# Cross-attention and an RWKV block: outputs reordered by small copies instead of turnings on TensorE, and more pairs of steps with a weighing between the score tiles

## The chip, the cores and the metric

One core of one Trainium2 chip. The metric is the device time of one launch in microseconds, lower is better; it is the median of several runs.

## What is computed

Batch 8, 256 tokens, width 256. First a cross-attention with 32 query heads and 8 key/value heads (head size 8) over 1601 context tokens, with output projection, residual and layer norm:

```python
q = x @ Wq + bq;  k = ctx @ Wk + bk;  v = ctx @ Wv + bv
scores = einsum('bkgld,bksd->bkgls', q, k) / sqrt(8) + mask        # mask is zero here
out = einsum('bkgls,bksd->bkgld', softmax(scores), v)
x = layernorm(out.reshape(b, l, 256) @ Wo + bo + x) * gamma + beta
```

Then an RWKV block per batch element: layer norm, token shift, low-rank mixes, products r, k, v, g, a decayed state `s = k v + w s` scanned over the 256 tokens for 32 heads, group norm, projection, and a channel mix with a squared relu and a sigmoid gate.

## The kernel before, in words

The program is written out by hand for each engine, with semaphores between them. It is a pipeline over the batch elements. In turn `it` five elements are at work: `f = it + 2` (its keys and values are projected), `a = it + 1` (its stacks of queries and keys are made), `b = it` (its scores, exp and weighing run), `c = it - 1` (output projection and the RWKV block up to the scan), `d = it - 2` (the channel mix's end). A letter is None where the element does not exist: `c` in turn 0, `f` in turns 6 and 7, `b` from turn 8 on, which is the tail.

A turn has 52 steps: four groups of heads (`GROUPS`) by 13 chunks of 128 keys (`NC`). In a step PE makes two score tiles (128 x 1024 each, two matmuls of 512 columns), ACT takes the exp of each (`exp_tile`), and PE weighs the values with them (`weigh`), adding a group's 13 steps up in PSUM bank 4 (`po`), where a head lies in nine rows: eight of output, one of the denominator. There are two PSUM buffers for score tiles, so a score tile waits for the exp of the tile two before it. `weigh` of a group's first step waits until DVE has copied the group before out of the bank (`keep_output` into `o_raw`, semaphore `o_kept`).

PE works in pairs of steps. In an ordinary pair both score tiles of the first step are issued, then the weighings of the two steps before, then both tiles of the second step, then the pair's side work (`side`). In a pair that stands in `LIGHT` each weighing stands between two score tiles. Where `c` is None every pair but step 0 and the two in `DIVIDED` is light.

Side work of `c` that matters here: step 4 the output product w_o, 10 the turned `xn`, 16 Wv, 20 Wk, 24 Wr, 26 Wg, 34 the gather of the scan; of `f`: `project_kv` at steps 30, 32 and 40, whose results DVE biases (`bias_kv`, `kv_biased`). After each group, PE turns `o_raw` (`turn_output`: four 128 x 128 transposes, at steps 22, 28, 42 and at step 0 of the next turn), and DVE normalises the turned tile (`norm_output`: a reciprocal of 16 denominators a row, four small products into `attn`). At step 2 PE turns `attn` (`turn_rows`), DVE copies it to `attn_t`, and w_o is applied at step 4.

SP issues nearly all DMAs, in the order in which its program lists them: at step 0 `load_stacks(b, 1)` and `load_x_rows(c)`, at step 4 the stores of `a`'s query and key parts, at 14 the shift of group half 1 (`shift_to_dram`, `shift_to_stack`), at 18 `spread_v(c)` (eight DMAs of 257 KB from SBUF to SBUF), at 20 the context and x_t of `f`, at 26 `load_stacks(a, 0)`, at 38 the shift of half 0, at 44 the mask.

Before turn 0, element 0 is projected, its parts are split and stored to DRAM (`store_k_parts`, `store_queries`), read back as stacks (`load_stack_half`), and a sub-round of scores gives the shift of the exponent, which goes through DRAM too. SP loads the context of element 1 before it issues these stores. POOL loads the weights that are needed from turn 1 on (`late_loads`) as soon as element 0's context has come.

## Time and profile before

| | |
|---|---|
| runs | 1173.62, 1179.3, 1179.63 us; median 1179.3 |
| the profiled execution | 1178.83 us, of which 1176.9 between its first and last instruction |
| PE | 1054.9 us busy |
| ACT | 860.3 us busy |
| DVE | 574.8 us busy |
| POOL | 309.0 us busy |
| mean granted TensorE clock | 0.952 of full speed |
| moved by DMA | 87.48 MB |

An engine's busy time is the sum over its instructions; idle time of an engine that is not the bottleneck costs nothing. Lines such as L795 are lines of the kernel; most of PE's matmuls share L795, since a helper issues them, and are told apart by what they write and read.

### The profile page before, as it was taken

The numbers are of one execution on the slowest core, as the hardware profiler recorded it, in microseconds if no ns is written. First come the engines' busy times: TensorE is split into PE (matmuls) and PEld (weight loads), VectorE is DVE, ScalarE is ACT, GpSimd is POOL, SyncE is SP. The second block draws the span as 40 slices with busy tenths as digits, with TensorE's granted clock in tenths as the row PEclk, the third lists the DMA queues.
The fourth block names the chain that finished last, engine by engine and source line by source line (L and its number), as shares of the span: only waits on it lengthen the run. The fifth ranks groups of instructions, "written<-read, shape, count | busy, mean of one in ns | idle before, by whom it ended". The sixth has DMA issues, their size and how long they took to land.

```text
span 1176.9 us, 18264 instructions
## 1 busy us (share of the span) xinstructions
PE 1054.9 (90%) x7181; PEld 376.0 (32%) x7181; DVE 574.8 (49%) x1095; ACT 860.3 (73%) x940; POOL 309.0 (26%) x356
## 2 busy tenths in 40 slices
PE   3198999999999999999999999999997999888777
PEld 2031223333333233323333333323331333224413
DVE  5031215464448445555547453844555364635562
ACT  2078988889878887888788988887788888881110
POOL 9221051232314041314123231314132012300330
PEclk8599999999999999999999999999999999998766
DMA  8534133631536140904253143614070225000400
GB/s 258 128 82 134 25 83 86 93 83 57 116 44 136 59 95 30 170 6 94 83 87 88 58 113 44 139 59 93 31 107 3 34 75 82 3 1 9 72 0 13
DMA packets 65374, 87.48 MB, mean 74 GB/s; under 512 B 8208, under 2 KB 48192, under 8 KB 65280
## 3 DMA queue, kind: packets, MB, share of 16 engines
q1 hardware_dynamic: 61728, 81.22, 31.6%
q0 software_dynamic: 2176, 4.11, 1.5%
q8 instruction: 59, 0.97, 0.3%
q10 hardware_dynamic: 1376, 0.90, 0.3%
q14 instruction: 35, 0.29, 0.1%
HBM read 50.74 MB, written 18.62 MB: 59 GB/s over the span
## 4 chain that ended last, share of the span: by engine, by line
PE 62%; ACT 23%; issue 6%; DVE 5%; DMA 3%; SPq 1%; POOL 0%; ACTq 0%; DVEq 0%; POOLq 0%
PE psum L795 61%; ACT probs L738 19%; DMA vs<-v_c 1%; DMA q_stacked<-q_parts 1%; ACT L738 1%; ACT L770 1%; PE psum L885 1%; SPq L291 1%; DVE xa L1336 1%; DMA q_stack<-q_stacked 1%; DVE row_max L1248 1%; DVE sx L1341 0%; ACT xm L767 0%; ACT xm L770 0%; SPq L367 0%
## 5 line engine op out<-in xcount | busy, mean ns | idle before, releaser
L738 ACT ACTIVATE probs<-psum 128x1024 f32<-128x1024 f32 (+1 forms) x832 | 798.9, 1022 | 199.8 <-PE psum L795 197.5
L795 PE MATMUL psum<-probs,v_aug 128*9 128x512 f32 (+1 forms) x3328 | 416.7, 599 | 1.3 <-DVE o_raw L1296 1.2
L795 PE MATMUL psum<-q_stack,k_stack 64*128 64x512 bf16 (+1 forms) x1745 | 320.5, 395 | 50.2 <-ACT probs L738 37.9
L795 PEld LDWEIGHTS psum<-q_stack,k_stack 64*128 64x128 bf16 (+1 forms) x1745 | 81.9, 96 | 440.5 <-ACT probs L738 359.5
L795 PEld LDWEIGHTS psum<-probs,v_aug 128*9 128x9 f32 (+1 forms) x3328 | 61.6, 89 | 161.2 <-issue 151.3
L599 POOL TENSOR_TENSOR vs<-r_c,vs 128x512 f32<-128x512 f32 x64 | 86.5, 1361 | 96.4 <-DVE tmp L1523 53.9
L576 POOL TENSOR_TENSOR xm<-tmp,xa 128x512 f32<-128x512 f32 x40 | 43.5, 1104 | 233.2 <-DVE tmp L1356 233.2
L1369 DVE TENSOR_TENSOR_SCAN vs<-w_c,vs 128x514 f32<-128x514 f32 x64 | 90.1, 1408 | 21.8 <-POOL vs L590 19.9
L563 POOL TENSOR_TENSOR rstd<-moments,eps 128x2 f32<-128x2 f32 x24 | 4.7, 195 | 255.8 <-DVE moments L1322 255.8
L1296 DVE COPY o_raw<-psum 128x512 f32<-128x512 f32 x32 | 21.9, 684 | 89.7 <-PE psum L795 89.7
L1362 DVE TENSOR_TENSOR vs<-k_c,vs 128x512 f32<-128x512 f32 x64 | 61.9, 967 | 0.3
L1356 DVE SCALAR_TENSOR_TENSOR tmp<-psum,chan,sx 128x256 f32<-128x256 f32 x80 | 33.5, 478 | 53.3 <-PE psum L795 53.3
L795 PE MATMUL psum<-ctx_t,w_kv 128*128 128x400 f32 (+1 forms) x128 | 50.1, 529 | 5.4 <-DMA ctx_t<-in_ctx_t 5.4
L535 POOL CAST k_parts<-kv 64x1601 bf16<-64x1601 f32 x7 | 10.6, 1519 | 121.0 <-DVE kv L1225 121.0
L1248 DVE TENSOR_REDUCE row_max<-psum 128x16 f32<-128x512 f32 x32 | 20.6, 684 | 41.8 <-PE psum L795 41.8
L1225 DVE TENSOR_SCALAR kv<-psum,b_kv 128x400 f32<-128x400 f32 (+1 forms) x28 | 17.6, 627 | 42.5 <-PE psum L795 42.5
L795 PE MATMUL psum<-k_stack,q_stack 48*128 48x32 bf16 x512 | 9.0, 174 | 30.9 <-DMA q_stack<-q_stacked 30.9
L795 PEld LDWEIGHTS psum<-ctx_t,w_kv 128*128 128x128 f32 x128 | 23.3, 195 | 25.2 <-issue 11.1
L1566 DVE RECIPROCAL xm<-xm 128x512 f32<-128x512 f32 x8 | 26.8, 3348 | 7.1 <-ACT xm L770 7.1
L1242 DVE TENSOR_REDUCE mask_max<-ctx_t 128x1 f32<-128x1601 f32 x16 | 28.7, 1806 | 0.0
L795 PE MATMUL psum<-mix,w 128*128 128x256 f32 (+1 forms) x64 | 18.0, 415 | 6.2 <-DVE mix L1345 6.2
L1285 DVE CAST shift_parts<-psum 32x128 bf16<-32x128 f32 x16 | 4.5, 279 | 38.8 <-PE psum L795 38.8
(181 smaller groups left out, 1061.8 us busy)
## 6 DMA issues: line engine op xcount, KB each, us to landing
vs<-v_c SPq DMA_DIRECT2D x61, 257.0 KB, 7.6
ctx_t<-in_mask SPq DMA_DIRECT2D x8, 1601.0 KB, 6.7
k_stacked<-k_parts SPq DMA_DIRECT2D x48, 200.1 KB
ctx_t<-in_ctx_t SPq DMA_DIRECT2D x24, 400.0 KB, 6.1
k_stack<-k_stacked SPq DMA_DIRECT2D x31, 300.2 KB, 6.6
q_stack<-q_stacked SPq DMA_DIRECT2D x31, 192.0 KB, 7.1
q_stacked<-q_parts SPq DMA_DIRECT2D x90, 64.0 KB, 3.1
ctx_t<-in_ctx_t SPq DMA_DIRECT2D x8, 401.0 KB, 6.4
```

What stands on the lines that cost most here:

```text
L576: nc.gpsimd.tensor_tensor(xm[MIX_ORDER[n]][:, :, :], tmp[n % 2][:, :, :], xa[:, :, 1:L + 1], ALU.add)\
L599: nc.gpsimd.tensor_tensor(vs[:, j, :, 0:L], r_c[:, :, :], vs[:, j, :, 0:L], ALU.mult)\
L738: nc.scalar.activation(probs[turn_step % NP][t][0:w, :, :], ps[t][0:w, :, :], ACT.Exp).then_inc(exped.sem, 1)
L795: return nc.tensor.matmul(dst, lhsT, rhs, start=start, stop=stop)
L1225: nc.vector.tensor_scalar(kv32[:, at:at + w], bank(at_bank)[:, 0:w], b_kv[:, 0:1], None, ALU.add)\
L1242: nc.vector.tensor_reduce(mask_max[:, a, lc:lc + 1], ctx_t[:, lc, :], AX.X, ALU.max, apply_absolute_value=True).then_inc(mask_seen.sem, 1)
L1248: last = nc.vector.tensor_reduce(row_max[:, :].rearrange("p (r a u) -> p r a u", a=2, u=4)[:, :, half, :], bank(6 + half).rearrange("p (r ...
L1296: nc.vector.tensor_copy(o_raw[:, :], po).then_inc(o_kept.sem, 1)
L1356: last = nc.vector.scalar_tensor_tensor(tmp[n % 2][:, e, :], halves(at)[:, e, :], vec(f"s{f}", e), sx[:, e, :], ALU.add, ALU.mult)
L1362: nc.vector.tensor_tensor(vs[:, j, :, 1:L + 1], k_c[:, :, :], vs[:, j, :, 1:L + 1], ALU.mult)\
L1369: nc.vector.tensor_tensor_scan(flat, w_c[:, :, :].rearrange("p e l -> p (e l)"), flat, 0.0, ALU.mult, ALU.add)\
L1566: link(nc.vector.reciprocal(std_o[:, :, :], std_o[:, :, :]))
```

## The change

The turned outputs and their normalisation in rows are gone. Instead SP copies each group's `o_raw`, with eight DMAs from SBUF to SBUF, head by head to rows of `attn_t`, and the denominators, spread over eight rows each, to rows of `den_t` (`turn_attn`). They are issued at steps 22, 30 and 42, and at step 0 of the next turn, ahead of what else SP has in those steps and behind what it has in earlier ones. `keep_output` waits for the group before to have been copied. Once a turn DVE takes the reciprocal of all denominators, their minimum (in place of the denominators kept for `count_over`), and multiplies (`norm_attn`). w_o is loaded with its rows in the order of `attn_t`.

`LIGHT` has seven pairs more: 4, 20, 22, 28, 30, 44, 50. The load of `x_rows` moves from step 0 to step 46 of the turn before. At the start SP issues element 0's stores and stack load before the context of element 1, ACT takes two of SP's query stores over, and POOL starts the late loads only when the first stacks have landed. Waits of PE for `o_normed` become waits for what else uses the bank.

```diff
-LIGHT = (2, 8, 10, 18, 38, 42, 48)
+LIGHT = (2, 4, 8, 10, 18, 20, 22, 28, 30, 38, 42, 44, 48, 50)
+ATTN_STEP = (22, 30, 42)
+FIRST_STORES = 2
...
+            def turn_attn(b, group):
+
+                if group == 0 and b > 0:
+                    sp.wait_ge(wo_done.sem, wo_done.at(b - 1))
+                sp.wait_ge(o_kept.sem, o_kept.at(b, group + 1))
+                for j in range(4):
+                    p0 = 32 * group + HD * j
+                    for dst, src in ((den_t, o_raw[32 * j + HD:32 * j + HD + 1, :].rearrange("p (a n) -> p a n", a=1)
+                                      .broadcast_to([1, HD, 512])),
+                                     (attn_t, o_raw[32 * j:32 * j + HD, :])):
+                        sp.dma_start(dst[p0:p0 + HD, :, :].rearrange("p h l -> p (h l)"), src).then_inc(attn_in.sem, 16)
...
-                sp.wait_ge(kv_proj.sem, kv_proj.at(lo))
-                load_ctx(lo + 1)
-                sp.wait_ge(q_proj.sem, q_proj.at(lo))
-                load_x_t(lo + 1)
...
                 store_k_parts(lo)
-                store_q_parts(lo, (1,))
+                sp.wait_ge(q_low.sem, q_low.at(lo))
+                store_queries(sp, lo, 1, range(FIRST_STORES, NR))
                 load_stacks(lo, 0, (0,))
+                sp.wait_ge(kv_proj.sem, kv_proj.at(lo))
+                sp.wait_ge(q_proj.sem, q_proj.at(lo))
+                load_ctx(lo + 1)
+                load_x_t(lo + 1)
...
                         if step == 0:
+                            if c is not None:
+                                turn_attn(c, 3)
                             if b is not None:
                                 load_stacks(b, 1)
-                            if c is not None:
-                                load_x_rows(c)
+                        if step in ATTN_STEP and b is not None:
+                            turn_attn(b, ATTN_STEP.index(step))
+                        if step == 46 and b is not None:
+                            load_x_rows(b)
...
+                if lo == 0:
+                    pool.wait_ge(stack_in[0].sem, stack_in[0].at(0))
+                    for dst, src in late:
+                        pool.dma_start(dst, src).then_inc(late_in.sem, 16)
...
-                    if step == 0:
-                        pe.wait_ge(o_normed.sem, o_normed.at(c, 3))
-                        turn_output(c, 3, 5)
-                    elif step == 2:
-                        pe.wait_ge(o_normed.sem, o_normed.at(c, 4))
+                    if step == 4:
...
-                        turn_rows(attn, 5, attn_turned)
-                    elif step == 4:
-                        pe.wait_ge(attn_kept.sem, attn_kept.at(c))
+                        pe.wait_ge(attn_normed.sem, attn_normed.at(c))
                         product_rows(attn_t, w_o, 5, wo_done)
...
             def keep_output(b, group):
                 dve.wait_ge(weighed.sem, weighed.at(b, NC * (group + 1)))
-                dve.wait_ge(o_turned.sem, o_turned.at(b, group))
+                if group > 0:
+                    dve.wait_ge(attn_in.sem, attn_in.at(b, 16 * HD * group))
+                elif b > 0:
+                    dve.wait_ge(attn_in.sem, attn_in.at(b - 1))
                 nc.vector.tensor_copy(o_raw[:, :], po).then_inc(o_kept.sem, 1)
...
+            def norm_attn(b):
+
+                dve.wait_ge(attn_in.sem, attn_in.at(b))
+                nc.vector.reciprocal(den_t[:, :, :], den_t[:, :, :]).then_inc(den_turned.sem, 1)
+                dve.wait_ge(den_turned.sem, den_turned.at(b))
+                nc.vector.tensor_reduce(den_low[:, b % B:b % B + 1], den_t[:, :, :], AX.XY, ALU.min)
+                nc.vector.tensor_tensor(attn_t[:, :, :], attn_t[:, :, :], den_t[:, :, :], ALU.mult)\
+                  .then_inc(attn_normed.sem, 1)
...
-                        norm_output(c, 3, 5)
-                        dve.wait_ge(attn_turned.sem, attn_turned.at(c))
-                        nc.vector.tensor_copy(attn_t[:, :, :], halves(5)).then_inc(attn_kept.sem, 1)
+                        norm_attn(c)
```

## Rows read from the trace of the kernel before

**Rows 1.** The page's chain of work that ended last, shares by engine.
```profile
PE 62%; ACT 23%; issue 6%; DVE 5%; DMA 3%; SPq 1%; POOL 0%; ACTq 0%; DVEq 0%; POOLq 0%
```
**Rows 2.** Busy time of each engine in one turn's window; columns in its first row.
```profile
core 0: us, PE busy (x) PEld busy (x) DVE busy (x) ACT busy (x) POOL busy (x), PEclk, DMA share, GB/s
562.80:690.40 127.60, 123.71 (x887) 44.73 (x887) 69.80 (x135) 106.40 (x116) 34.84 (x36) 1.00 0.38 81
```
**Rows 3.** PE in order of time: start, duration (us), instruction, idle before it and its releaser.
```profile
612.23 0.66 PE L885 MATMUL psum<-ident,o_raw 128*128 128x128 f32 x4
...
623.13 1.90 PE L795 MATMUL psum<-probs,v_aug 128*9 128x512 f32 x16
...
634.79 1.61 PE L795 MATMUL psum<-ctx_t,w_kv 128*128 128x400 f32 x4
...
690.60 0.39 PE L795 MATMUL psum<-q_stack,k_stack 64*128 64x512 bf16 x2 [0.48 <-ACT probs L738]
...
693.78 1.99 PE L795 MATMUL psum<-w_o,attn_t 128*128 128x256 f32 x8
```
**Rows 4.** Groups by line and shape: busy us and mean ns, then idle before.
```profile
L1566 DVE RECIPROCAL xm<-xm 128x512 f32<-128x512 f32 x8 | 26.8, 3348 | 7.1 <-ACT xm L770 7.1
...
L1310 DVE TENSOR_TENSOR attn<-psum,r_den 128x32 f32<-128x32 f32 x128 | 15.5, 184 | 1.1
...
L1464 DVE TENSOR_TENSOR x<-x,rows 128x512 f32<-128x512 f32 x8 | 5.5, 692 | 0.3
```
**Rows 5.** SP in order of time, in turn 4: start and duration of DMA issues.
```profile
562.45 0.60 SPq L291 DMA_DIRECT2D q_stacked<-q_parts  x1
...
588.50 0.33 SPq L385 DMA_DIRECT2D shift_stacked<-shift_parts  x1
...
597.71 14.85 SPq L304 DMA_DIRECT2D vs<-v_c  x8
612.68 4.61 SPq L351 DMA_DIRECT2D ctx_t<-in_ctx_t  x4
617.33 0.86 SPq L354 DMA_DIRECT2D x_t<-in_x_t  x1
618.36 0.91 SPq L284 DMA_DIRECT2D k_stack<-k_stacked  x1
```
**Rows 6.** DMA issues in 563 to 691 us: KB each, us from issue to landing.
```profile
out<-y_out SPq DMA_DIRECT2D x1, 256.0 KB, 2.2
x_t<-in_x_t SPq DMA_DIRECT2D x1, 256.0 KB, 7.9
...
shift_stacked<-shift_parts SPq DMA_DIRECT2D x2, 24.0 KB, 1.4
```
**Rows 7.** DVE in order of time.
```profile
620.39 0.68 DVE L1296 COPY o_raw<-psum 128x512 f32<-128x512 f32 x1
...
634.04 0.61 DVE L1225 TENSOR_SCALAR kv<-psum,b_kv 128x401 f32<-128x401 f32 x1
...
683.19 0.69 DVE L1296 COPY o_raw<-psum 128x512 f32<-128x512 f32 x1 [4.39 <-PE psum L795]
```
**Rows 8.** PE in order of time, in turn 0.
```profile
94.12 1.90 PE L795 MATMUL psum<-probs,v_aug 128*9 128x512 f32 x8 [1.20 <-DVE o_raw L1296]
```
**Rows 9.** Window of 3 us behind it; columns as in rows 2.
```profile
94.00:97.00 3.00, 2.88 (x14) 0.39 (x18) 0.00 (x0) 0.78 (x2) 0.00 (x0) 0.50 0.49 156
```
**Rows 10.** The chain that ended last, at the start: start and duration in us.
```profile
30.70 9.09 DMA q_stacked<-q_parts
...
40.31 6.58 DMA q_stack<-q_stacked
```
**Rows 11.** The start in order of time.
```profile
17.84 5.01 SPq L367 DMA_DIRECT2D k_stacked<-k_parts  x6
...
56.12 1.04 PE L795 MATMUL psum<-q_stack,k_stack 64*128 64x512 bf16 x4 [6.25 <-issue]
```
**Rows 12.** The tail in order of time.
```profile
1065.17 0.69 DVE L1296 COPY o_raw<-psum 128x512 f32<-128x512 f32 x1 [3.60 <-PE psum L795]
...
1070.66 3.78 PE L795 MATMUL psum<-w_o,attn_t 128*128 128x256 f32 x8 [0.78 <-DVE attn_t L1452]
```

More of the change, by code:

```diff
@@ L287, in load_stack_half, with store_queries @@
                           q_st_d[n % B][4 * k0:4 * k0 + 8].rearrange("h r d l -> (r d) h l")).then_inc(stack_in[g].sem, 16)
-        def store_queries(eng, a, c):
-            for r, n in enumerate(Q_PARTS):
-                eng.dma_start(q_st_d[a % B][16 * c:16 * c + 16, r], q_parts[:, n, c, :]).then_inc(q_out.sem, 16)
+        def store_queries(eng, a, c, parts=range(NR)):
+            for r in parts:
+                eng.dma_start(q_st_d[a % B][16 * c:16 * c + 16, r], q_parts[:, Q_PARTS[r], c, :]).then_inc(q_out.sem, 16)
         def spread_done(c, j):
@@ L313, in late_loads @@
             c = dram
-            yield w_o[:, :, :], c["L0_xattn_Wo"].rearrange("(c p) n -> p c n", p=P)
+            wo_attn = c["L0_xattn_Wo"].rearrange("(g j u h d) n -> g u h j d n", g=GQ, j=4, u=2, h=GQ)
+            for group in range(GROUPS):
+                for h in range(GQ):
+                    yield w_o[32 * group:32 * group + 32, h, :], wo_attn[group // 2, group % 2, h]
             for n, name in enumerate(["L0_xattn_bo", "L0_xattn_gamma", "L0_xattn_beta"]):
@@ L367, in store_k_parts, with store_q_parts @@
                     sp.dma_start(k_st_d[a % B][:, r], k_parts[:, n, :]).then_inc(k_out.sem, 16)
-            def store_q_parts(a, chunks=range(EC)):
+            def store_q_parts(a):
                 sp.wait_ge(q_low.sem, q_low.at(a))
-                for c in chunks:
+                for c in range(EC):
                     store_queries(sp, a, c)
@@ L678, in _ @@
             pool.wait_ge(cleared_up.sem, 1)
-            pool.wait_ge(ctx_in[NK - 1].sem, ctx_in[NK - 1].at(0))
-            for dst, src in late:
-                pool.dma_start(dst, src).then_inc(late_in.sem, 16)
             all_turns(0)
@@ L726, in project @@
                 store_queries(act, a, 0)
+                store_queries(act, a, 1, range(FIRST_STORES))
                 act.wait_ge(cleared.sem, 1)
@@ L880, in weigh @@
                 last.then_inc(weighed.sem, 1)
-            def turn_output(b, group, to):
-                pe.wait_ge(o_kept.sem, o_kept.at(b, group + 1))
-                for u in range(4):
-                    last = nc.tensor.transpose(bank(to)[:, P * u:P * u + P], o_raw[:, P * u:P * u + P], ident[:, :])
-                last.then_inc(o_turned.sem, 1)
             def turn_rows(x, to, done):
@@ L940, in score_rows @@
                         else:
[L941 removed]
+                            pe.wait_ge(shift_kept[1].sem, shift_kept[1].at(b))
                         if general:
@@ L1032, in side @@
                             pe.wait_ge(kv_biased.sem, kv_biased.at(f, 2))
-                        elif b is not None:
-                            pe.wait_ge(o_normed.sem, o_normed.at(b, 2))
                         else:
@@ L1124, in side @@
                         if n == 0:
-                            pe.wait_ge(o_normed.sem, o_normed.at(b, 2))
+                            if c is not None:
+                                pe.wait_ge(k_ready.sem, k_ready.at(c))
+                            else:
+                                pe.wait_ge(v_kept.sem, v_kept.at(a))
                         elif n == 1:
@@ L1294, in keep_output @@
                 dve.wait_ge(weighed.sem, weighed.at(b, NC * (group + 1)))
-                dve.wait_ge(o_turned.sem, o_turned.at(b, group))
+                if group > 0:
+                    dve.wait_ge(attn_in.sem, attn_in.at(b, 16 * HD * group))
+                elif b > 0:
+                    dve.wait_ge(attn_in.sem, attn_in.at(b - 1))
                 nc.vector.tensor_copy(o_raw[:, :], po).then_inc(o_kept.sem, 1)
-            def norm_output(b, group, at):
-                g, pair = group // 2, group % 2
-                dve.wait_ge(o_turned.sem, o_turned.at(b, group + 1))
-                t = bank(at).rearrange("p (h c j d) -> p h c j d", h=2, c=LC, d=32)
-                den = r_den[:, b % B, group, :]
-                link(nc.vector.reciprocal(den.rearrange("p (u j) -> p u j", j=4),
-                                          bank(at).rearrange("p (u j d) -> p u j d", j=4, d=32)[:, :, :, HD]))
-                if group == 0 and b > 0:
-                    dve.wait_ge(attn_turned.sem, attn_turned.at(b - 1))
-                for hd in range(2):
-                    for lc in range(LC):
-                        u = LC * hd + lc
-                        last = nc.vector.tensor_tensor(
-                            attn[:, lc, P * g:P * g + P].rearrange("p (j h d) -> p j h d", h=G, d=HD)[:, :, 2 * pair + hd, :],
-                            t[:, hd, lc, :, 0:HD],
-                            den[:, 4 * u:4 * u + 4].rearrange("p (j d) -> p j d", d=1).broadcast_to([P, 4, HD]), ALU.mult)
-                last.then_inc(o_normed.sem, 1)
+            def norm_attn(b):
[5 more added lines that the diff above has]
+                  .then_inc(attn_normed.sem, 1)
             def row_moments(x, c, n):
@@ L1508, in all_turns @@
                         mix_of(c, 4)
-                    if b is not None:
-                        norm_output(b, 0, 6)
                     if c is not None:
@@ L1526, in all_turns @@
                         state_pass(c, 4)
-                    if b is not None:
-                        norm_output(b, 1, 5)
                     if c is not None:
@@ L1573, in all_turns @@
                           .then_inc(og_ready.sem, 1)
-                    if b is not None:
-                        norm_output(b, 2, 5)
                     if c is not None:
```

38 lines of the change are left out of this document (8 added, 30 removed).

## The prediction, made before the change was run

> **What bounds the kernel now.** I read the chain of waits first: nearly two thirds of the span lies on PE and a quarter on ACT [rows 1]. The window cut at one turn (52 steps, 127.6 us) says the same: PE 123.71 us busy, ACT 106.40 [rows 2]. So a turn ends 3.9 us above PE's own work. There are eight turns with scores (`it` 0 to 7) and a tail; turns 1 to 7 are much like this one. PE's order of time [rows 3] shows where part of the 3.9 us lies: where a pair of steps issues both score tiles at once after a light pair, the second waits for exp. There are four such waits a turn, in pairs 4, 20, 44 and 50, of 0.2 to 0.5 us, 1.4 together (0.48 at 690.60, pair 4, is the largest). The rows are of turn 4, from 553.1 to 680.7, and the start of turn 5; the `weigh` at 623.13 is that of step 26, the first of output group 2.
>
> **What is removed.** Five turnings a turn. One takes at most 0.66 us of PE [rows 3]; I take 0.55 on its queue. Those of pairs 0, 22 and 28 stand in pairs that PE bounds: 1.6 us. The one in pair 42 and `turn_rows` in pair 2 stand where PE waits for exp next: nothing. On DVE four normalisations go, each with four products of 184 ns and a small reciprocal [rows 4], some 0.7 us. Seven more light pairs move no work, and can at best take the 1.4 us of waits. Together 3.0 us a turn, if nothing new is waited for.
>
> **What is added on DVE, once a turn.** A reciprocal of 128x512, 3.35 us, and a multiplication, 0.69 us [rows 4]; the minimum I take like the multiplication, 0.7 (bounds 0 and 1.8; it stands between the two). In all 4.7 us, and PE's w_o product waits for it.
>
> **What is added on SP: eight copies per group**, 256 in all. SP issues a copy in 0.33 (the shift's) to 0.60 us (a store) [rows 5]; I take 0.45, 3.6 us for eight, bounds 2.7 and 5.1. Alone, a copy lands 1.4 us (the shift's) or 2.2 us (y_out's) after its issue [rows 6]; I take 2.2.
>
> *Group 3, pair 4.* o_raw is kept at 683.19 + 0.69 = 683.9 [rows 7]. Then 3.6 + 2.2 + 4.7 gives 694.4. The product began at 693.78 [rows 3]; PE, freed of a turning and a wait, could now be there near 692.9. So it is 0.6 us later than before, and what pairs 0 to 4 gave is absorbed. Bounds: at 2.7 + 1.4 nothing is waited for; at 5.1 + 2.5 it is 2.4 us late. I take +0.3, below the midpoint of what the sum says and nothing, since the minimum is the softest of its terms. DVE's next work, keep_v and x0, is waited for only by later products.
>
> *Groups 1 and 2* are copied with over 20 us to the next keep: hidden. load_stacks, the stores and x_rows move 3 to 4 us on SP, and nobody waits for them that closely.
>
> *Group 0, step 22, is the place that decides.* SP takes its queue in order: the eight spreads of v (597.71, 14.85 us), then the context load (612.68, 4.61) and x_t (617.33, 0.86), and only then the new copies, from 618.2, where load_stacks is issued now [rows 5]. `keep_output(b, 1)` may not overwrite o_raw before they have landed. It runs at 620.39 now [rows 7], and PE weighs step 26 at 623.13 only after it; all of PE is queued behind that. When do the copies land?
> - The floor: 618.2 + 8 x 0.34 + 1.4 = 622.3.
> - The queue is not empty. x_t, 256 KB, landed 7.9 us after its issue, at 625.2; y_out, of the same size, alone, in 2.2 [rows 6]. The difference is the 1.6 MB ahead of it. Copies issued behind x_t on the same queue I put behind it: 626.
> - The ceiling: issue slowed as for the first stack there (0.91 us) gives some 628.
>
> On this the Trainium skill has two rules. "DMA: Bandwidth & Descriptors", section "Anatomy of one DMA", gives a DMA of GpSimd's path a fixed cost of about 2.0 us, and a small one little beside it: taken for SP's too, the copies land at 621.8 + 2.0 = 623.8, an estimate, and the sum would be that of the short wait below. The same page's "Queues, rings and completion order" says that each DMA engine takes descriptors in ring order: by it 626 and the sum below. The 7.9 us of x_t agree with the second.
>
> With 626, keep_output ends at 626.75 against 621.07: DVE is 5.7 us late, less the 0.7 of `norm_output(b, 1)`: 5.0. PE's projection at 634.79 started just after the kv_biased that DVE began at 634.04 [rows 3, 7], so PE is at least 5.0 late there. By its own queue PE is 626.8 - 623.13 = 3.7 late, less the turning of pair 28: 3.2, plus what the clock takes: after a wait of PE for o_raw that ended at 94.12 [rows 8] the granted clock was 0.50 over the next 3 us [rows 9], which is the lower of its two levels, 1.2 and 2.4 GHz, and worth 1.5 to 3 us of work here. That makes 4.7 to 6.2; I take 5.5. The savings of pairs 20 to 28 are swallowed, since SP's queue starts from v_ready at step 16. Left are pairs 44 and 50 (-0.7) and pair 4 (+0.3): **+5.1 us a turn**, in turns 1 to 5, where c and f both exist: **+25.5**. At the floor it is 1.3 - 0.4 = +0.9 a turn; at the ceiling DVE is 7.0 late, less the same 0.4: +6.6.
>
> Turns 6 and 7 load no context, and the spreads' backlog ends near the deadline. There the savings show: -3.0 and +1.3 (the part absorbed at pair 4) = -1.7 each, **-3.5**. Turn 0 has no c and most of its pairs are light already: 0.
>
> **Start.** Now SP's last stores queue behind the next context, and the last lands 9.09 us after its issue, at 39.8; the stacks land 6.58 us after theirs, at 46.9 [rows 10]. After: the stores start where k's do now, 17.84 [rows 11], ten on SP at 0.64 (0.60 and the gap) end at 24.2, ACT's eight near 25; landed by 28.5 at the latest that I can justify (2.2 and one more for the 2 MB), stacks 7 us later, 36: -11. But the context, 1.9 MB with x_t, is then queued ahead of the shift's small copies, which stand between the stacks and the first scores at 56.12, and 4 MB of late loads start beside them: +2.5. **-8.5**, bounds -5 and -11.
>
> **Tail.** o_raw is kept at 1065.17 + 0.69; turnings and copies let the product start at 1070.66 [rows 12]. Now 3.6 + 2.2 + 4.7 = 10.5: 1076.4. Nothing covers it: 5.7, **+6** with the clock, bounds +4 and +8.
>
> **Sum** against the profiled execution's own 1178.8 (span 1176.9 and 1.9 around it; the median of the runs is 1179.3, 0.5 above, which I leave): 1178.8 - 8.5 + 25.5 - 3.5 + 6 = **1198**. With the bounds of its terms, copies landing from 625 to 628, this case runs from 1188 to 1212.
>
> **Rivals.**
> - *Short wait*: the eight small copies are not held by the context and land near 623.8. DVE is 2.8 late, PE as much with a little clock: 2.4 a turn with the same -0.4, 12 in all: 1185 (1173 at the floor of every term). For it: the copies are small. Against: x_t's 7.9 us. Chance 0.2.
> - *In time, so faster*: the copies land before 621.3, at which keep_output costs PE nothing. Then each of turns 1 to 7 gives 1.7: 1178.8 - 8.5 - 12 + 6 = 1164. It needs SP to reach them 1 us or more earlier than it reaches load_stacks now. For it: SP's spreads are slow because its queue is full, and x_rows no longer stands in it. Against: 14.85 us of spreads ahead, which the change leaves alone. Chance 0.17.
> - *The normalisation binds, not group 0*: 2.4 instead of 0.3 at pair 4, 2.1 x 7 = 15 on top of 1164: 1179. It decides from an issue of 0.6 us a copy. For it: eight issues, where one is measured. Against: 0.33 for the one most like them. Chance 0.13.
> - The likeliest, 0.5.
>
> **Chances.** No change that a measurement can tell is within 0.5%, 1173 to 1185. Faster: 0.17 and a little of the short wait and the third, 0.21. Same: half the short wait and most of the third, 0.18. Slower: the likeliest and the rest, 0.61. The range 1168 to 1211 leaves out most of the 1164 case and the worst of the ceiling, about 2 in 10.
>
> **What would show it.** In the trace after: PE waiting for o_raw at step 26 in turns 1 to 5, 2 to 5 us each, and a clock under 1.00 behind it; no such wait in turns 6 and 7; turns 1 to 5 near 133 us, turn 6 near 126; first scores at 47 to 48; the tail's w_o product some 10.5 us after the last keep. The prediction is wrong if SP's copies at step 22 land within 3 us of their issue, or if a turn falls under 127.6.

## The result, and the profile after

After takes **1219.9 us** (median of 4 runs, 1216.14 to 1225.84), before 1179.5 beside it (1173.62 to 1179.75): ratio **1.0355, 95% interval 1.0314 to 1.0395**. The change makes the kernel slower, by twice what was predicted (+19.5), and the time lies above the range of 1168 to 1211. The profiled execution of after took 1218.04 us, 1215.9 of them span, 39.0 more than before's 1176.9.

The page's chain that ended last, shares by engine, to be held against [rows 1]:
```profile
PE 45%; ACT 18%; issue 16%; DVE 10%; SPq 5%; DMA 4%; POOL 2%; ACTq 1%; POOLq 0%; DVEq 0%
```
The share on PE has fallen from 62 to 45%, and SP's queue and DMAs have risen from 4 to 9%: the end now hangs on copies for part of every turn. The window that answers to [rows 2], turn 4:
```profile
core 0: us, PE busy (x) PEld busy (x) DVE busy (x) ACT busy (x) POOL busy (x), PEclk, DMA share, GB/s
577.97:711.61 133.64, 123.63 (x869) 42.20 (x870) 71.96 (x117) 106.56 (x117) 36.11 (x36) 0.99 0.38 82
```
PE is as busy as before, 123.63 us, in a turn 6.0 us longer. So the turn is lost in PE's waits. Two are new; PE in order of time, with the projection that answers to the last-but-two of [rows 3]:
```profile
582.72 1.99 PE L819 MATMUL psum<-w_o,attn_t 128*128 128x256 f32 x8 [2.44 <-DVE attn_t L1299]
...
643.00 1.90 PE L819 MATMUL psum<-probs,v_aug 128*9 128x512 f32 x8 [3.84 <-DVE o_raw L1291]
...
656.25 1.61 PE L819 MATMUL psum<-ctx_t,w_kv 128*128 128x400 f32 x4 [0.30 <-DVE kv L1217]
```
The second was predicted, the first only as 0.3 us. What leads to them, DVE and then SP in order of time (the same places as [rows 5] and [rows 7]):
```profile
570.53 0.69 DVE L1291 COPY o_raw<-psum 128x512 f32<-128x512 f32 x1 [4.25 <-PE psum L819]
...
577.99 3.35 DVE L1296 RECIPROCAL den_t<-den_t 128x512 f32<-128x512 f32 x1 [3.61 <-DMA attn_t<-o_raw]
581.38 0.69 DVE L1298 TENSOR_REDUCE den_low<-den_t 128x1 f32<-128x512 f32 x1
581.98 0.68 DVE L1299 TENSOR_TENSOR attn_t<-attn_t,den_t 128x512 f32<-128x512 f32 x1
...
642.16 0.69 DVE L1291 COPY o_raw<-psum 128x512 f32<-128x512 f32 x1 [5.35 <-DMA attn_t<-o_raw]
```
```profile
571.25 0.65 SPq L416 DMA_DIRECT2D den_t<-o_raw  x1
...
576.00 0.63 SPq L416 DMA_DIRECT2D attn_t<-o_raw  x1
...
614.30 14.68 SPq L306 DMA_DIRECT2D vs<-v_c  x8
629.09 5.04 SPq L356 DMA_DIRECT2D ctx_t<-in_ctx_t  x4
634.17 0.47 SPq L359 DMA_DIRECT2D x_t<-in_x_t  x1
634.74 0.73 SPq L416 DMA_DIRECT2D den_t<-o_raw  x1
...
639.61 0.63 SPq L416 DMA_DIRECT2D attn_t<-o_raw  x1
```
*Group 3*: kept at 570.53, eight copies issued from 571.25 to 576.63, one every 0.67 us where 0.45 was taken; landed 577.99, 1.4 after the last; then 3.35 + 0.69 + 0.68 on DVE, and the product at 582.72, where PE had stood ready for 2.44 us. *Group 0*: issued from 634.74 to 640.24, landed 642.1, and DVE's copy of group 1, which had 5.35 us of idle time ahead of it, comes 35.4 us after that of group 0, and 30.3 before. After PE's wait the clock is at the lower of its two levels:
```profile
643.00:646.00 3.00, 3.00 (x16) 0.39 (x20) 1.25 (x3) 0.52 (x1) 2.27 (x2) 0.52 1.15 166
```
Turn 6 has no context load, yet waits too; SP, then DVE:
```profile
905.16 0.63 SPq L416 DMA_DIRECT2D attn_t<-o_raw  x1
...
907.24 0.69 DVE L1291 COPY o_raw<-psum 128x512 f32<-128x512 f32 x1 [1.44 <-DMA attn_t<-o_raw]
```
The start in order of time, all engines ([rows 10] and [rows 11] show it before):
```profile
31.58 0.34 SPq L286 DMA_DIRECT2D k_stack<-k_stacked  x1
...
38.50 0.61 PE L819 MATMUL psum<-k_stack,q_stack 48*128 48x32 bf16 x32 [21.22 <-DMA q_stack<-q_stacked]
...
50.58 1.03 PE L819 MATMUL psum<-q_stack,k_stack 64*128 64x512 bf16 x4 [9.24 <-issue]
```
The stacks are there 8.5 us earlier than in [rows 10], but from them to the first scores it takes 12.1 us, and 9.1 before. The tail, in order of time ([rows 12] before):
```profile
1100.12 0.69 DVE L1291 COPY o_raw<-psum 128x512 f32<-128x512 f32 x1 [3.50 <-PE psum L819]
...
1107.57 3.35 DVE L1296 RECIPROCAL den_t<-den_t 128x512 f32<-128x512 f32 x1 [4.14 <-DMA attn_t<-o_raw]
...
1112.30 3.78 PE L819 MATMUL psum<-w_o,attn_t 128*128 128x256 f32 x8 [10.32 <-DVE attn_t L1299]
```

The 32 copies to o_raw divide both traces at the same places of the work. From their starts (us; before and after):

| stretch | predicted | measured |
|---|---|---|
| start and turn 0, to the last copy (174.60, 169.42) | -8.5 | -5.2 |
| turns 1 to 5 (to 810.84, 839.54) | +25.5 | +33.9 |
| turns 6 and 7 (to 1065.17, 1100.12) | -3.5 | +6.3 |
| tail (to the end of the spans) | +6 | +4.1 |
| sum | +19.5 | +39.0 |

### The profile page after: what moved, and what is told of

Its sections match the earlier page's. It is cut to its first block, busy times and chain, and to the rows that moved or that the text cites. A ratio compares the mean times of both kernels' runs of the same rounds, so it can differ in the third digit from the quotient of the medians.

```text
span 1215.9 us, 18031 instructions
## 1 busy us (share of the span) xinstructions
PE 1057.2 (87%) x7021; PEld 356.5 (29%) x7021; DVE 589.9 (49%) x951; ACT 860.2 (71%) x940; POOL 322.1 (26%) x363
## 4 chain that ended last, share of the span: by engine, by line
PE 45%; ACT 18%; issue 16%; DVE 10%; SPq 5%; DMA 4%; POOL 2%; ACTq 1%; POOLq 0%; DVEq 0%
PE psum L819 44%; ACT probs L762 15%; SPq L416 3%; DVE den_t L1296 2%; DMA vs<-v_c 2%; DMA attn_t<-o_raw 1%; SPq L306 1%; DVE vs L1348 1%; ACT L762 1%; ACT L794 1%; POOL vs L621 1%; ACTq L293 1%; DVE xa L1322 1%; DVE o_raw L1291 1%; DVE row_max L1240 1%
## 5 line engine op out<-in xcount | busy, mean ns | idle before, releaser
L819 PE MATMUL psum<-probs,v_aug 128*9 128x512 f32 (+1 forms) x3328 | 435.5, 612 | 19.7 <-DVE o_raw L1291 19.6
L819 PE MATMUL psum<-q_stack,k_stack 64*128 64x512 bf16 (+1 forms) x1745 | 331.9, 399 | 50.0 <-ACT probs L762 33.9
L819 PEld LDWEIGHTS psum<-q_stack,k_stack 64*128 64x128 bf16 (+1 forms) x1745 | 85.3, 95 | 487.5 <-ACT probs L762 378.3
L1355 DVE TENSOR_TENSOR_SCAN vs<-w_c,vs 128x514 f32<-128x514 f32 x64 | 102.3, 1598 | 21.9 <-POOL vs L612 20.0
L598 POOL TENSOR_TENSOR xm<-tmp,xa 128x512 f32<-128x512 f32 x40 | 46.0, 1165 | 234.0 <-DVE tmp L1342 234.0
L819 PEld LDWEIGHTS psum<-probs,v_aug 128*9 128x9 f32 (+1 forms) x3328 | 57.2, 89 | 166.2 <-issue 157.6
L1348 DVE TENSOR_TENSOR vs<-k_c,vs 128x512 f32<-128x512 f32 x64 | 54.6, 853 | 0.3
L819 PE MATMUL psum<-w_o,attn_t 128*128 128x256 f32 x64 | 20.7, 479 | 28.6 <-DVE attn_t L1299 28.6
L1296 DVE RECIPROCAL den_t<-den_t 128x512 f32<-128x512 f32 x8 | 26.8, 3353 | 32.6 <-DMA attn_t<-o_raw 32.6
```

The lines of the kernel that those rows point to most:

```text
L598: nc.gpsimd.tensor_tensor(xm[MIX_ORDER[n]][:, :, :], tmp[n % 2][:, :, :], xa[:, :, 1:L + 1], ALU.add)\
L819: return nc.tensor.matmul(dst, lhsT, rhs, start=start, stop=stop)
L1296: nc.vector.reciprocal(den_t[:, :, :], den_t[:, :, :]).then_inc(den_turned.sem, 1)
L1348: nc.vector.tensor_tensor(vs[:, j, :, 1:L + 1], k_c[:, :, :], vs[:, j, :, 1:L + 1], ALU.mult)\
L1355: nc.vector.tensor_tensor_scan(flat, w_c[:, :, :].rearrange("p e l -> p (e l)"), flat, 0.0, ALU.mult, ALU.add)\
```

## The experiments

Where a stage is named by two copies, as "group 0 to 1", it is the time between their starts; a turn goes from one copy of group 3 to the next. Ratios are to the kernel before on the same chip.

### Parts of the change alone

**The new light pairs on the kernel before.**
```diff
-LIGHT = (2, 8, 10, 18, 38, 42, 48)
+LIGHT = (2, 4, 8, 10, 18, 20, 22, 28, 30, 38, 42, 44, 48, 50)
```


> The kernel before with the seven new light pairs and nothing else. My sum gives them at best the 1.4 us of waits for exp a turn: 10 us in seven turns, 1169, and the pairs whose side work is long should lose nothing since PE bounds them. The rival: in a heavy light pair ACT has one tile instead of two to work on during the side work, falls behind and is waited for in the next pair; then the time rises, 0.5 to 1.5 us a turn, 1183 to 1190, and this is part of what the change lost in turns 6 and 7.

1174.77 us, ratio 0.9973 (0.9960 to 0.9985). PE waits 27.8 us for ACT in all, 37.9 before. Group 3 to 0 takes 34.2 for 34.6, group 2 to 3 30.35 for 30.60, and the turn is 0.6 us shorter in turns 2, 3 and 5: under half of the 1.4 that the waits held. Turn 4 is 1.0 us longer than before's. Turn 5 from copy to copy, before and then here (columns as in [rows 2]):
```profile
683.19:810.84 127.65, 123.58 (x889) 44.77 (x889) 69.92 (x135) 106.63 (x117) 34.84 (x37) 1.00 0.38 81
```
```profile
683.75:810.82 127.07, 124.44 (x889) 44.41 (x889) 69.95 (x135) 106.79 (x117) 34.86 (x37) 1.00 0.38 82
```
The four waits for exp of that turn (0.48, 0.25, 0.21 and 0.47) are all gone, and no other stands in their place. But PE is busy 0.86 us longer with the same 889 instructions: the sixteen matmuls of two weighings take 1.90 us in a row, and 1.04 for each eight where a score tile stands between them.

**The new order of the start on the kernel before.**
```diff
+                sp.wait_ge(q_low.sem, q_low.at(lo))
+                store_queries(sp, lo, 1, range(FIRST_STORES, NR))
                 load_stacks(lo, 0, (0,))
                 sp.wait_ge(kv_proj.sem, kv_proj.at(lo))
...
                 load_ctx(lo + 1)
```


> The kernel before with the new order of the start alone (stores and stacks ahead of the next context, two stores on ACT, late loads after the stacks). The trace of the changed kernel had its first scores 5.5 us earlier: if nothing is given back later, 1174. If the late loads delay turn 0 or the shift's copies further, the time stays at 1179.

1174.69 us, ratio 0.9977 (0.9961 to 0.9993). In the trace the first scores come 4.7 us earlier than before (51.44 for 56.12), and the last copy of turn 0 6.5 us earlier; by the ratio 2.7 us of it are left at the end (0.8 to 4.6).

**Both together on the kernel before**, that is the change without its turnings part.

> The kernel before with the two parts of the change that don't concern the turnings: the new light pairs and the new order of the start. Each alone gave 0.997. Theory (they add up, since they are in different places): 1172. What the kernel of 1165.25 (five copies, step 16) lies under this is what the removed turnings give once nothing waits for their replacement, 7 us: the predicted 1.3 to 1.7 a turn less the tail. Rival (the start's gain is absorbed in turn 0 when the light pairs are new): 1175 and no more than each alone.

1173.81 us, ratio 0.9951 (0.9933 to 0.9969). The ratios add up (0.9973 and 0.9977 make 0.9950), though the intervals are nearly as wide as the parts. The traces don't show it stage by stage: the last copy of turn 0 is at 172.88 here, at 168.12 with the start alone and at 174.60 before. All of after's loss, and more, is in the replacement of the turnings.

**After with the old light pairs.**

> The changed kernel with the light pairs of before. If the light pairs gain 0.7 us a turn in pairs 44 and 50 as I summed, it is 5 us slower than the changed kernel, 1225. If light pairs next to a long wait of PE starve ACT (weighing of step 26 ahead of the second score tile), it is faster: 1 to 2 us a turn, 1206 to 1213.

1225.89 us, ratio 1.0409 (1.0388 to 1.0430) against 1.0355 (1.0314 to 1.0395), so the new light pairs don't slow after; PE's waits for ACT are 53.2 us with the old, 33.9 with the new. They aren't the cause.

### Group 0's copies

**Issued at step 16, ahead of the spreads.**
```diff
-ATTN_STEP = (22, 30, 42)
+ATTN_STEP = (16, 30, 42)
```


> The changed kernel with the copies of group 0 at step 16, ahead of the spreads of v, instead of step 22, behind them and the context. If DVE's wait for these copies is what turns 1 to 5 lose between the keeps of groups 0 and 1 (5.2 us each; 1.3 in turns 6 and 7), the wait for them is gone and the time falls by 5 x 5.2 + 2 x 1.3 = 28 us plus what the clock loses, to 1190. The rival, that the many small copies slow the spreads and loads by contention wherever they stand, keeps it above 1205.

1196.83 us, ratio 1.0160 (1.0142 to 1.0178). Group 0 to 1 takes 30.0 us in each of turns 1 to 5, for 35.3 in the mean in after and 30.3 in before: the predicted wait is gone. But the kernel is still slower than before. The product with w_o waits as in after, and now the clock falls behind it in every turn. PE in turn 4, and the 3 us around it:
```profile
570.12 3.43 PE L819 MATMUL psum<-w_o,attn_t 128*128 128x256 f32 x8 [2.41 <-DVE attn_t L1299]
```
```profile
570.00:573.00 3.00, 2.88 (x7) 2.34 (x8) 2.40 (x3) 0.00 (x0) 0.00 (x0) 0.50 1.14 231
```
The product takes 3.43 us where it took 1.99 in after's turn 4. Group 3 to 0 is 36.9 to 39.1 us, for 36.2 in most turns of after and 34.6 before. So part of what one wait's removal gave went to the clock behind the other.

**The context issued behind the copies** (step 24 instead of 20).
```diff
-                        if step == 20 and f is not None:
+                        if step == 24 and f is not None:
```


> After's kernel; only the next context and x_t are issued at step 24, behind group 0's copies instead of ahead of them. In turn 4 the copies would be issued from 629.1 to 634.5. Theory A (the queue is the order of issue, and a copy lands 1.9 us after it): landed 636.4, DVE's wait of 5.3 falls to nothing, 5 turns x 5.3 + clock: 1219.9 - 27 = 1193, near the 1196.8 of the kernel with step 16. Theory B (the spreads' bytes hold them too; a spread lands 7.4 us after its issue): landed 637.5 to 639, wait 1 to 2.5 left, 1200 to 1207. In both the w_o wait of 2.4 stays.

1198.08 us, ratio 1.0190 (1.0158 to 1.0222), between the two theories: the copies land right behind their issue, as in A, but a wait of 1.3 to 1.5 is left, the size that B had. SP, DVE and PE in turn 4:
```profile
615.72 1.61 SPq L416 DMA_DIRECT2D den_t<-o_raw  x1
617.38 1.98 SPq L416 DMA_DIRECT2D attn_t<-o_raw  x1
...
622.76 0.63 SPq L416 DMA_DIRECT2D attn_t<-o_raw  x1
```
```profile
624.83 0.69 DVE L1291 COPY o_raw<-psum 128x512 f32<-128x512 f32 x1 [1.50 <-DMA attn_t<-o_raw]
```
```profile
569.23 1.99 PE L819 MATMUL psum<-w_o,attn_t 128*128 128x256 f32 x8 [2.43 <-DVE attn_t L1299]
```
The last was issued by 623.4 and DVE went on 1.4 us later, the least that [rows 6] show for a small transfer: here the bound is the issue itself. Right behind the spreads the first two issues take 1.6 and 2.0 us instead of 0.65, as in after's turn 6, where the same 1.44 us are waited for. On PE the wait shows as 1.3 us ahead of the projection, whose operand DVE makes after that copy. PE waits for the product's operand as long as in the kernel with step 16, yet here the product takes 1.97 to 1.99 us in turns 1 to 6, and only in turn 7 2.7.

**Five copies instead of eight**: the four of the denominators are one.
```diff
+                sp.dma_start(den_t[32 * group:32 * group + 32, :, :].rearrange("p h l -> p (h l)"),
+                             o_raw[HD:P:32, :].rearrange("p (a n) -> p a n", a=1).broadcast_to([4, HD, 512]))\
+                  .then_inc(den_in.sem, 16)
```


> As the last, and the four copies of the denominators are one, whose source is the four partitions of one group: five copies for eight, the same bytes. Theory A (the issue on SP sets the time, 0.67 us a copy, and each lands about 1.9 after it, whatever is queued from the context): the copies of group 0 land 2.0 us earlier, DVE's wait for them falls from 5.3 to 3.3, the w_o wait is gone, the tail's is 7.5 to 8; 1219.9 - 5 x 4.2 - 2 x 3.4 - 3 = 1189. Theory B (they land behind x_t, as predicted before the run: x_t lands at 640.7 in turn 4, the copies after it): group 0 gives 0.5 at most, and the time is 1197 to 1199. Theory C (one copy with four times the bytes costs four times the issue): as the last kernel, 1202.

1205.00 us, ratio 1.0247 (1.0212 to 1.0282): none of the three theories. ("The last" is the kernel with the denominators first and a count of their own, shown below.) The w_o wait is gone, and so is the wait of turns 6 and 7, but group 0 to 1 in turns 1 to 5 takes 36.9 to 39.9 us, more than in after. SP, DVE, and windows of 2 us:
```profile
631.22 0.47 SPq L360 DMA_DIRECT2D x_t<-in_x_t  x1
631.78 0.66 SPq L412 DMA_DIRECT2D den_t<-o_raw  x1
632.48 2.80 SPq L417 DMA_DIRECT2D attn_t<-o_raw  x4
635.45 0.33 SPq L287 DMA_DIRECT2D k_stack<-k_stacked  x1
```
```profile
642.32 0.69 DVE L1295 COPY o_raw<-psum 128x512 f32<-128x512 f32 x1 [8.21 <-DMA attn_t<-o_raw]
```
```profile
636.00:638.00 2.00, 0.47 (x3) 0.10 (x2) 0.00 (x0) 1.07 (x2) 0.00 (x0) 1.00 1.03 228
638.00:640.00 2.00, 0.00 (x0) 0.00 (x0) 0.00 (x0) 0.00 (x0) 0.00 (x0) 1.00 1.16 142
640.00:642.00 2.00, 0.00 (x0) 0.00 (x0) 0.00 (x0) 0.00 (x0) 0.00 (x0) 0.76 1.06 176
```
The last copy was issued by 635.3 and landed 7 us later; all engines of the core stood still for 4 us, while the DMA engines were full. The issue of the copies now ends well before the context has landed (x_t lands 7.9 us after 631.22, by the median of this kernel), and the next turn's stacks are issued right behind them.

**The same with the stack loads later**, once group 1 is kept.
```diff
+                        if step == 30 and a is not None:
+                            if b is not None:
+                                sp.wait_ge(o_kept.sem, o_kept.at(b, 2))
+                            load_stacks(a, 0)
...
-                        if step == 26 and a is not None:
-                            load_stacks(a, 0)
```


> The kernel with five copies a group (group 0 at step 22, behind the context), in which DVE waited 8.2 us for group 0's copies in turn 4 although the last was issued 2.0 us earlier than in after's kernel. Here the four stack loads of the next turn, issued right behind those copies until now (635.45 in turn 4), wait until output group 1 has been kept. Theory A (the stack loads' bytes, of many small packets, share the engines with the last copies and hold them): the copies land with x_t, near 6.5 to 8 us after x_t's issue; DVE's wait falls from 8.2 to 3.5 to 4.5, 5 turns x 4: 1205 - 20 = 1185. Theory B (the one wide copy is itself slow behind a context, whoever comes after it): the waits stay at 7 to 8 and the time at 1203 to 1207.

1192.86 us, ratio 1.0111 (1.0089 to 1.0133), 12 us less than with the stacks behind the copies (16 by the ratios); the wait of turn 4 is 5.9 instead of 8.2, in turns 1 to 5 5.8 instead of 7.7 in the mean. SP, DVE, and the windows:
```profile
627.17 0.47 SPq L360 DMA_DIRECT2D x_t<-in_x_t  x1
...
628.55 2.74 SPq L417 DMA_DIRECT2D attn_t<-o_raw  x4
```
```profile
635.52 0.69 DVE L1297 COPY o_raw<-psum 128x512 f32<-128x512 f32 x1 [5.92 <-DMA attn_t<-o_raw]
```
```profile
630.00:632.00 2.00, 1.96 (x10) 1.20 (x8) 0.00 (x0) 1.54 (x2) 0.00 (x0) 1.00 0.99 326
632.00:634.00 2.00, 0.00 (x0) 0.00 (x0) 0.00 (x0) 1.02 (x1) 0.00 (x0) 1.00 0.32 110
634.00:636.00 2.00, 0.00 (x0) 0.00 (x0) 0.48 (x1) 0.00 (x0) 0.00 (x0) 0.93 0.02 6
```
The last copy was issued by 631.3, but DVE goes on at 635.5, 4.2 us later and 7.9 after x_t's issue had ended. x_t lands 6.7 us after its issue in this kernel (median), at 633.9, and the copies' landing is 1.6 after that; in after it is 6.5, 640.7, and 1.4. So the copies land behind x_t, and finishing their issue 2 us sooner gained nothing: this is the predicted backlog. Where nothing lies ahead, the wide copy lands 2.3 us after its issue and the small ones 1.4 (group 3), so the 4.2 aren't explained by the copies themselves. The DMA engines are full only until about 632.5, though; what the last copies wait for in the 3 us behind that, the runs don't show. Theory A was right that the stack loads hold the copies too, and wrong in what remains without them: it had 3.5 to 4.5 us.

### Group 3's copies and the product with w_o

**The four copies of the denominators first, with a count of their own.**
```diff
-                dve.wait_ge(attn_in.sem, attn_in.at(b))
+                dve.wait_ge(den_in.sem, den_in.at(b))
                 nc.vector.reciprocal(den_t[:, :, :], den_t[:, :, :]).then_inc(den_turned.sem, 1)
...
+                dve.wait_ge(attn_in.sem, attn_in.at(b))
                 nc.vector.tensor_tensor(attn_t[:, :, :], attn_t[:, :, :], den_t[:, :, :], ALU.mult)\
                   .then_inc(attn_normed.sem, 1)
```


> After's kernel; only the order of a group's eight copies changes: the four of the denominators first, with a count of their own, so that group 3's reciprocal need not wait for the four of the numerators (which land 2.7 us later). Theory (the w_o wait of 2.4 us a turn is the chain keep, eight issues of 0.67, landing, 3.35 + 0.7 + 0.7 on DVE, and nothing else is behind it): the wait falls to 0 to 0.3 us, turns 1 to 7 give 2.2 each and the tail 2.6: 1219.9 - 18 = 1202. Rival (something else holds that place, ACT or the later keep for instance, and the wait only moves to another instruction): within 5 us of 1220, with the same turn period of 133.6.

1196.82 us, ratio 1.0187 (1.0151 to 1.0223). PE's waits, in us in total, times and the longest:
```profile
PE psum L823 <- DVE attn_t L1306: 8.8, 2, 7.8
```
In after they are 28.6 us in 8 times. Only the tail's is left, and 1.0 in one turn. Group 3 to 0 is 33.7 us. So the chain of keep, issues, landing and DVE's three operations was all that held the product: nothing took its place. It gave 23 us by the medians and 20 by the ratios, for 18 expected. In the traces 18.9 of it lie in turns 1 to 7, where 15.4 had been expected and where the clock no longer falls behind the wait, and 5.5 in the tail; that although group 0 to 1 grew by 0.9 us in turns 1 to 5 (36.2 in the mean for 35.3).

### Both waits taken away

**Five copies, group 0's at step 16.**

> The five copies, and group 0's issued at step 16 instead of 22, ahead of the spreads. Theory (the two waits, at group 0 and ahead of w_o, are all that the change costs in a turn; the removed turnings then show): turns of 126.2 to 126.6 us, 1.0 to 1.4 under before's, start -5, tail +1.5: 1177.6 - 9 - 5 + 1.5 = 1165. Rival (copies ahead of the spreads delay the state passes that wait for the spreads, and the turn gives it back there): turns of 127.6 or more, 1174 to 1180.

**1165.25 us, ratio 0.9903 (0.9873 to 0.9934)**, 1% faster than before, clear of the noise. Its window for turn 4, DVE and PE:
```profile
551.35:677.32 125.97, 122.40 (x869) 42.28 (x870) 71.86 (x118) 106.53 (x117) 36.13 (x36) 1.00 0.40 87
```
```profile
547.68 3.34 DVE L1300 RECIPROCAL den_t<-den_t 128x512 f32<-128x512 f32 x1
...
551.66 0.68 DVE L1304 TENSOR_TENSOR attn_t<-attn_t,den_t 128x512 f32<-128x512 f32 x1
...
553.60 1.99 PE L821 MATMUL psum<-w_o,attn_t 128*128 128x256 f32 x8
```
The product finds its operand 1.3 us before it comes to it. The turn is 126.0 us, 1.6 under before's, PE 122.40 us busy, 1.3 less than in [rows 2]. The rival is out: the turn gives nothing back behind the spreads.

**Eight copies with the denominators first, group 0's at step 16.**

> Eight copies with the denominators first, and group 0's at step 16: what the single wide copy adds to the best kernel so far (1165.25). With eight, DVE's reciprocal starts 2.7 + 1.9 us after the keep instead of 0.7 + 1.9, and the multiplication may not start before the eighth has landed: the w_o product waits 0 to 0.3 us a turn, and in the tail 1.2 to 2 more than with five: 1165 + 1 to 4 = 1166 to 1169. Rival (eight copies in a row anywhere on SP cost the turn as much as at step 22): 1180 or more.

1167.72 us, ratio 0.9890 (0.9867 to 0.9913): the intervals of the two overlap, so the single wide copy isn't shown to be worth anything there. What counts is the step, and that the reciprocal waits for the denominators alone. Each of these two gave 23 us by itself; together they give 52. The 6 us above their sum lie where the kernel with step 16 alone is slower than after: group 3 to 0 takes it 263.2 us in turns 1 to 7 and after 255.9, with the clock falling behind the wait in seven turns instead of three.

**The late loads behind the first shift**, on the kernel with five copies.
```diff
-                    pool.wait_ge(stack_in[0].sem, stack_in[0].at(0))
+                    pool.wait_ge(shift_in[0].sem, shift_in[0].at(0))
```


> The kernel of 1165.25 us (five copies, group 0's at step 16); only the late loads wait for the shift's copies of the first turn instead of for its stacks. In that kernel 13.3 us lie between the stacks' landing (38.3) and the first scores (51.58), and 9.1 in the kernel before. Theory A (the 4 MB of late loads, started at 38.7, hold the shift's two small copies): 9.1 to 10 us, the first scores at 47.5 to 48.5, and 3 to 4 us off the time: 1161.5. Theory B (the next context and x_t, 1.9 MB issued before the shift, hold them): 12 to 13 us as now, 1165. The rows of the kernel show a DMA share of 1.0 at 38 to 44, which either could fill.

1167.63 us, ratio 0.9917 (0.9896 to 0.9939), not told apart from 0.9903 and no gain. Theory A was right on the place and wrong on the time. PE's first scores, then what POOL and DVE did:
```profile
47.94 1.04 PE L821 MATMUL psum<-q_stack,k_stack 64*128 64x512 bf16 x4 [6.14 <-issue]
```
```profile
76.96 0.54 POOL L650 DMA_DIRECT2D s_init<-in_s_init  x1
77.49 0.52 POOL L548 COPY v_aug<-v_st 128x384 f32<-128x384 f32 x1
```
```profile
78.25 0.69 DVE L1228 COPY v_st<-psum 128x512 f32<-128x512 f32 x1 [6.50 <-POOL v_aug L552]
```
The scores start 3.6 us earlier (47.94 for 51.58), 9.0 after the stacks: the late loads did hold the shift. But POOL issues them one by one until 77.5, and its copy of v stands behind them; DVE waits 6.5 us for it. By the first copy to o_raw the kernel is 3.3 us behind the other (91.59 for 88.31).

## Why the prediction was right in direction and half the size

**The step that failed** is "*Group 3, pair 4* ... I take +0.3", with the term "I take 0.45, 3.6 us for eight" under it. An issue of such a copy takes 0.63 to 0.73 us and comes every 0.67: 5.4 us for eight, above the bound of 5.1. The landing took 1.4 after the last, not 2.2, and DVE's three operations 4.7 as taken. So the product starts 11.5 us after the group is kept and not 10.5, PE stands 2.4 us for it (0.8 of these are savings in the pairs before), and the place is 1.6 us later than before in the turns in which the clock holds; the sum had given 0.6, and halving it to 0.3 because a term was soft took away what was true. For the issue I took a value between the shift's 0.33 and the stores' 0.60, both for another kind of copy; the upper bound was the nearer. The second half of the mistake is that the wait was given no clock: where PE had to wait, the product itself took 2.6 to 3.6 us instead of 2.0 in some turns. And the third rival, which named this wait and its condition of 0.6 a copy, had it *instead of* group 0's, while the two lie in series in one turn: the true case was their sum.

How much hangs on it: between the copies of group 3 and group 0, turns 1 to 7 take 17.7 us more than before's, 2.5 a turn, where the prediction had 0.3 a turn, 2.1 in all. The kernel with the denominators first takes 21.0 us less than after there, and from the last copy of turn 0 to that of turn 7 18.9 less (911.8 us, 170.85 to 1082.66, for 930.7). Held against a kernel without this wait, as that one is, the prediction's own figure is 1.3 a turn, 9 in all: the 0.3, and the 1.0 of savings in pairs 0 to 4 that it called absorbed.

By stage, over turns 1 to 5, from the copies' starts:

- *Group 3 to 0* (pair 4): predicted +1.5, measured +12.5. Three turns are at +1.4 to +1.6; turn 1 (where PE waits 3.5 us) is at +4.7 and turn 5 at +3.2, where the clock falls behind the wait: the product takes 3.57 and 2.64 us there instead of 1.99. The prediction had given this wait no clock.
- *Group 0 to 1*: predicted +27.5, measured +25.1. The copies landed at 642.1, which is 625.5 on before's scale (shifted by 16.6 us, the difference of the group 0 copies); 626 had been predicted, and DVE's and PE's waits (5.35, 3.84) and the clock of 0.52 came as described. That the number fits is in part luck. The prediction had the issue end at 621.8 and the copies wait 4 us more for what lies ahead of them. In after the issues alone nearly give the landing: in turns 1, 2, 3 and 5 it follows the last issue by 1.5 to 1.6 us, in turn 4 (640.24) by 1.9, and where no context lies ahead by 1.4. The last copy lands 2.5 us after its issue began (639.61), within the 3 us that the prediction had named as a sign that it is wrong. The backlog is there too: in the kernel with five copies and the stacks later, copies issued by 631.3 land 7.9 us behind the end of x_t's issue, for 7.5 in after. The two bounds happened to fall within a microsecond of each other; with the 0.45 us an issue that had been assumed, the issue would have ended near 638.3, and the backlog would have set the landing. Of the Trainium skill's two rules ("DMA: Bandwidth & Descriptors"), that of "Queues, rings and completion order", descriptors taken in ring order, agrees with copies that in turn 4 land 1.5 us after x_t in after and 1.6 in the kernel with the stacks later, by x_t's median, whenever their issue ends; with the stacks right behind them it is 3.2. The 2.0 us that the Trainium skill gives in "Anatomy of one DMA" of the same page fit after itself (by estimate 640.24 and 2.0, 642.2, for 642.1), but would have had the copies land at 637.3, an estimate too, in the kernel with five copies (635.3, where the last issue ends, and 2.0), where the trace has 642.3; where no bulk lies ahead the traces have 1.4.
- *The rest*: predicted -3.5, measured -3.7, but not in its places. The -3.5 were the waits of pairs 44 and 50, which lie between groups 2 and 3; there it is -1.5, and -2.2 between groups 1 and 2, where nothing had been put.

**Turns 6 and 7**: predicted -3.5, measured +6.3: +5.2 from group 3 to 0, +2.5 from group 0 to 1, -1.5 in the rest. With the denominators first they come to -2.2 (830.56 to 1082.66, for 810.84 to 1065.17), so 8.5 of the 9.8 us go with the chain to w_o: 5.3 between group 3 and 0, the rest in later parts of the turns, which wasn't followed. The wait of 1.44 us at group 0, where "the spreads' backlog ends near the deadline", is the issue's again: eight of them, the first two slowed.

**The savings** were put at 3.0 us a turn once nothing new is waited for. The kernel of 1165.25 us, which has no such wait, shows 1.6: 0.5 from the light pairs (the kernel with these and the new start goes from its copy at 172.88 to that at 806.86, 2.3 under before in five turns), and 1.2 from the turnings (167.77 to 795.85, another 5.9 less). The light pairs' 1.4 was an upper bound taken as the value, under a premise that failed, that they "move no work": the waits went, but PE's own time rose by 0.86 us a turn. The turnings take 2.0 us off PE (124.44 to 122.40), but waits for exp of 0.46 and 0.20 us are there again, and 1.6 had been put for them. In after this was hidden under the waits.

**The start**: predicted -8.5, measured -5.2. Stacks 8.5 us earlier, not 11: SP's ten stores, taken at 0.64 us each as in [rows 11], took 6.3 for six and 4.4 for four, 1.1 each, so that the stack load was issued at 31.58. The stores went out as ACT's did; that this slowed them is the likely reason, and was not tried. Then +3.0 for the crowded shift, where +2.5 was taken. The late loads are the cause of that (last experiment). Among the kernels with after's start the first scores come between 50.0 and 52.6, so a single trace tells this stage to 1 or 2 us only; 47.94, with the late loads behind the shift, lies outside.

**The tail**: predicted +6, measured +4.1. The product starts 11.5 us after the last group is kept, for the 10.5 of the sum. That the end is 2 us nearer than the sum wasn't followed: the two kernels with the denominators first have the same program there and differ by 5.2 us (110.2 and 115.4).

**The rivals.** "In time" is excluded: the copies needed until 642.1, and with the context ahead they do even when issued sooner. The short wait is excluded by its time, less by its mechanism: in after the context holds the copies by 0.5 us at most, and the rival had the wait short because it took 0.45 us an issue, as the likeliest case did. "The normalisation binds" was right with its condition, an issue of 0.6 us. Its price of 2.4 was a delay against before; that delay is 1.4 to 1.6 in the four turns in which the clock holds (2, 3, 4 and 6) and comes to 2.5 in the mean only by turns 1, 5 and 7, so the price fits by luck.

**The signs that had been named.** PE's wait in turns 1 to 5 and the clock behind it came, and these turns took 133.5 to 135.4 us. In turns 6 and 7 PE doesn't wait for o_raw, as forecast, but DVE waits 1.4 us for the copies. Turn 6 took 131.0 us and not 126, the first scores came at 50.6 and not 47 to 48, and the tail's product came 11.5 us after the last keep and not 10.5.

The error of 19.5 us is made of +3.3 (start), +8.4 (turns 1 to 5), +9.8 (turns 6 and 7) and -2.0 (tail). The step that failed makes up 15.6 of it: 17.7 us between groups 3 and 0 in turns 1 to 7, for 2.1.

## What to carry to other kernels

Work that goes from an engine's few microseconds to eight small DMAs is paid on the issuing queue, one issue after the other, before the first byte counts; when the consumer is near, order the copies by who needs them first and give the first ones a count of their own. Place copies that free a buffer ahead of the bulk traffic of their queue, not behind it, and look at what is issued right behind them as well. And two new waits of one turn are in series: rivals that can both be true need a case of their own, in which their prices, and what the clock does behind each, are added.

## What the runs showed of the hardware that was not expected

- An SBUF-to-SBUF copy of 16 KB costs SP 0.63 to 0.75 us of issue in all but eight of after's 256, one of 64 KB with four source partitions 0.57 to 0.65 in the kernel of 1165.25 us: the price doesn't grow with the bytes. Behind the eight spreads the first two take 1.6 and 2.0 us.
- Small copies can land later when fewer are issued: with five instead of eight the landing moved from 1.9 to 7.0 us after the last issue, and as a time from x_t's issue from 8.0 to 11.1. Moving the stack loads, which are issued behind them, took 2.3 us of DVE's wait away: a DMA that is issued later delays one issued before it.
- A wait of PE of 2.4 us is sometimes followed by the lower clock and sometimes not. In after the product takes 2.6 to 3.6 us instead of 2.0 in turns 1, 5 and 7 (waits of 3.5, 2.4 and 2.6 us), with group 0's copies at step 16 2.8 to 3.8 in every turn. That PE waits 3.84 us elsewhere in after's turn and not in that kernel doesn't decide it: with the context later PE has the wait of 2.4 and elsewhere one of 1.3 only, and the product takes 1.99. The runs don't show what does.
